# Beginning of a six-layer local-attention kernel: clearings, mask, x copies, softplus and input statistics placed elsewhere

## What is computed

```
xn = (x - mean) / sqrt(var + 1e-5)
s  = recurrent_branch(xn)            # log_alpha = -8 * softplus(forget_base) * sigmoid(forget)
for i in range(6):
    t = attn(shift_tokens(t), Wqkv[i], ...) + t    # 16 heads of 64, window 32, masked softmax
    t = ffn(shift_tokens(t), ...) + t              # layer norm, gated GELU
out = x + s * silu(t)
```

## Time and profile before

| what | value |
|---|---|
| median of three runs | 1648.02 us |
| the profiled execution | 1647.35 us |
| its span in the profile | 1645.6 us |
| busy: PE, PEld | 97%, 83% |
| busy: DVE, ACT, POOL | 83%, 82%, 80% |
| mean granted clock of TensorE | 0.998 of full speed |
| the chain that ended last | PE 81%, DVE 7%, ACT 4%, POOL 3%, issue 3% |

### The profile page before, as it was taken

One profiled execution on the slowest core, in us unless ns is written; L12 is line 12 of the kernel. 1 busy time (PEld: TensorE's weight loads), 2 busy tenths in 40 slices (PEclk: granted clock), 3 DMA queues, 4 the chain that ended last, 5 costly groups with the idle time before them and its releaser, 6 DMA issues.

```text
span 1645.6 us, 50851 instructions
## 1 busy us (share of the span) xinstructions
PE 1592.4 (97%) x19920; PEld 1367.4 (83%) x19920; DVE 1368.5 (83%) x2011; ACT 1343.9 (82%) x2518; POOL 1322.8 (80%) x1283
## 2 busy tenths in 40 slices
PE   5899999999999999999999999999999999999997
PEld 3678888888888888888888888888888888888786
DVE  6888888888888888888888888888888888888865
ACT  5768888788888888888888888888888888878884
POOL 8988898888889888889888889878888776677742
PEclk9999999999999999999999999999999999999999
DMA  4345233433323344232344333334333332222231
GB/s 135 99 119 140 71 98 85 119 108 98 107 76 90 102 116 120 77 106 76 100 113 114 99 83 99 84 105 132 86 94 87 92 85 69 77 73 69 64 113 33
DMA packets 184871, 156.89 MB, mean 95 GB/s; under 512 B 111550, under 2 KB 156092, under 8 KB 184636
## 3 DMA queue, kind: packets, MB, share of 16 engines
q1 hardware_dynamic: 184636, 153.64, 33.4%
HBM read 27.56 MB, written 1.05 MB: 17 GB/s over the span
## 4 chain that ended last, share of the span: by engine, by line
PE 81%; DVE 7%; ACT 4%; POOL 3%; issue 3%; DMA 0%; SPq 0%; POOLq 0%; ACTq 0%; DVEq 0%
PE ps_pv L793 12%; PE ps_s L769 10%; PE ps_pv L812 9%; PE ps_tr L730 9%; PE ps_qn L702 8%; PE ps_qn L703 7%; PE ps_qn L704 7%; PE ps_tr L714 5%; PE ps_pv L802 3%; PE ps_s L752 2%; PE ps_qn L892 2%; PE ps_qn L893 2%; PE ps_qn L894 2%; DVE ss L1542 1%; POOL qk L1968 1%
## 5 line engine op out<-in xcount | busy, mean ns | idle before, releaser
L1968 POOL TENSOR_TENSOR qk<-qk,t 128x1024 f32<-128x1024 f32 x192 | 455.8, 2376 | 92.8 <-DVE qk L1532 92.6
L1529 DVE TENSOR_TENSOR t<-ps_qn,tab 128x512 f32<-128x512 f32 x384 | 264.6, 689 | 129.3 <-ACT sq L1128 116.4
L1980 POOL TENSOR_TENSOR qkr<-qk,rinv 128x1024 f32<-128x1024 f32 x192 | 361.7, 1905 | 7.7 <-POOL rinv L1960 0.4
L1115 ACT ACTIVATE pbd<-ps_tr 64x512 f32<-64x512 f32 x384 | 226.0, 589 | 63.9 <-PE ps_tr L714 60.9
L702 PE MATMUL ps_qn<-w_hi,xs_hi 128*128 128x512 f32 x576 | 260.3, 452 | 16.4 <-DVE qk L1532 7.5
L1532 DVE TENSOR_TENSOR qk<-ps_qn,tab 128x512 f32<-128x512 f32 x384 | 261.5, 681 | 0.0
L1128 ACT ACTIVATE sq<-ps_qn 128x512 f32<-128x512 f32 x384 | 228.6, 596 | 35.8 <-PE ps_qn L704 31.1
L1161 ACT ACTIVATE qbd<-ps_tr 64x512 f32<-64x512 f32 x384 | 226.8, 591 | 32.7 <-PE ps_tr L730 27.2
L703 PE MATMUL ps_qn<-w_lo,xs_hi 128*128 128x512 f32 x576 | 229.2, 398 | 0.0
L704 PE MATMUL ps_qn<-w_hi,xs_lo 128*128 128x512 f32 x576 | 228.6, 397 | 0.0
L1542 DVE TENSOR_REDUCE ss<-sq 128x32 f32<-128x2048 f32 x96 | 216.6, 2256 | 0.0
(11 more groups left out here) (168 smaller groups left out, 3206.1 us busy)
## 6 DMA issues: line engine op xcount, KB each, us to landing
v_own<-v_new SPq DMA_DIRECT2D x96, 512.0 KB, 3.2
v_back<-v_new SPq DMA_DIRECT2D x96, 384.0 KB, 3.5
v_back<-v_own SPq DMA_DIRECT2D x94, 128.0 KB, 2.3
kT<-kT SPq DMA_DIRECT2D x84, 128.0 KB, 2.7
w_raw<-in_Wqkv SPq DMA_DIRECT2D x18, 512.0 KB, 5.2
rot<-in_rot SPq DMA_DIRECT2D x48, 128.0 KB, 2.6
fx<-xmid SPq DMA_DIRECT2D x96, 64.0 KB, 2.1
xsh<-x SPq DMA_DIRECT2D x190, 32.0 KB, 2.6
```

What stands on the lines that cost most here:

```text
L1529: v.tensor_tensor(t2[:, part].rearrange("p (h s d) -> p h s d", s=2, d=DH // 2), swapped, tab[:, 2 * k + 1:2 * k + 2, :].rearrange("p o (s ...
L1968: g.tensor_tensor(qk[b][:, part], qk[b][:, part], t2[:, part], ALU.add).then_inc(added[b], 1)
L1980: g.tensor_tensor(qkr[b][:, part].rearrange("p (h d) -> p h d", d=DH), qk[b][:, part].rearrange("p (h d) -> p h d", d=DH), rinv[b][:, k * ...
```

## The change

What it does:
- **Loads.** x comes in three parts instead of two: tiles 0 and 1 first as before, tiles 2 and 3 before the weights, tiles 4 to 7 between the k and the v part. The rotary table and the scales are issued before the k part instead of behind it.
- **Input statistics.** Columns 4 to 7 are taken after the first moments and before `input_root(0)`; columns 8 to 11 after the second rotation of half (0,0); columns 12 to 15 at the end of (0,0), with the moments of all twelve there as before.
- **x copies.** `copy_pair` is ScalarE's instead of VectorE's: pair 0 in (1,0) before `normalise_pair(1)`, pair 1 in (1,1) at the same place, pair 2 at the end of (1,1).
- **Mask.** The two conversions to bf16 are done by ScalarE in (0,1) (`round_mask`, after the copies of values) instead of by GpSimd in (0,0).
- **Clearings.** `clear_recurrent` follows `clear`, before GpSimd's first `split_first`.
- **Softplus.** Its size is taken by GpSimd at the end of (2,1) instead of (0,1), its exponential by ScalarE in (3,0) instead of (1,0), its reciprocals by VectorE in (3,1) instead of (1,1).

```diff
-        x_in, ... = [sem(f"x_loaded{q}") for q in range(2)], ...
+        x_in, ... = [sem(f"x_loaded{q}") for q in range(3)], ...
...
                 load_x(0, 2, 0)
                 sp.dma_start(rec.par[:, :, :], a["rec_par"]).then_inc(rec_par_in, 16)
                 sp.dma_start(ident[:, :], a["ident"]).then_inc(s_const, 16)
+                load_x(2, 4, 1)
                 w.load_wqkv(sp, 0, 0)
-                w.load_wqkv(sp, 0, 1)
                 w.load_rot(sp, 0)
                 w.load_scales(sp, 0)
+                w.load_wqkv(sp, 0, 1)
+                load_x(4, TILES, 2)
                 w.load_wqkv(sp, 0, 2)
-                load_x(2, TILES, 1)
...
# ScalarE
-                    act.wait_ge(s_st, 2 * (HEAD if g == 0 else COLUMNS))
+                    act.wait_ge(s_st, 2 * (COLUMNS if g else HEAD))
...
+                def copy_pair(r):
+                    bank, tokens = in_pair(r)
+                    act.wait_ge(s_tr, HEAD * (r + 2))
+                    f(x[:, :, tokens].rearrange("p b (t d) -> p t b d", d=P),
+                      bank[:, :].rearrange("p (t b d) -> p t b d", t=2, b=B), ACT.Copy).then_inc(s_xT, 1)
...
+                def round_mask():
+                    act.wait_ge(mask_in, 2 * 16)
+                    f(mask_bf[:, :, :], fc[:, :, :], ACT.Copy).then_inc(mask_ready, 1)
+                    f(sel_bf[:, :], fsq[:, 0, :], ACT.Copy).then_inc(mask_ready, 1)
...
                     if (i.n, b) == (1, 0):
+                        copy_pair(0)
                         normalise_pair(1)
+                    if (i.n, b) == (3, 0):
                         softplus_exp()
+                    if (i.n, b) == (1, 1):
+                        copy_pair(1)
...
+                    if (i.n, b) == (0, 1):
+                        round_mask()
                     if (i.n, b) in ((0, 1), (1, 0)):
                         normalise_pair(2 * i.n)
+                    if (i.n, b) == (1, 1):
+                        copy_pair(2)
...
# VectorE
-                    dve.wait_ge(s_st, 2 * (HEAD if g == 0 else COLUMNS))
+                    dve.wait_ge(s_st, 2 * COLUMNS if g else 3 * HEAD)
...
+                        if i.first and (b, c) == (0, 1):
+                            input_stats(range(8, 12), 2)
...
-                    if (i.n, b) == (1, 1):
-                        copy_pair(1)
+                    if (i.n, b) == (3, 1):
                         softplus_recip()
...
-                        input_stats(range(HEAD, COLUMNS), 1)
+                        input_stats(range(12, COLUMNS), 2)
                         input_moments(range(HEAD, COLUMNS), HEAD + COLUMNS)
-                    elif (i.n, b) == (1, 0):
-                        square_sums(i, b)
-                        copy_pair(0)
...
-                    if (i.n, b) == (1, 1):
-                        copy_pair(2)
...
                 input_stats(range(HEAD), 0)
                 input_moments(range(HEAD), HEAD)
+                input_stats(range(HEAD, 8), 1)
                 input_root(0)
...
# GpSimd
-                    if (i.n, b) == (0, 0):
-                        mask_constants_bf()
-                    elif (i.n, b) == (0, 1):
+                    if (i.n, b) == (2, 1):
                         softplus_size()
-                        clear_recurrent()
...
                 clear()
+                clear_recurrent()
                 for c in range(3):
                     split_first(c)
```

More of the change, by code:

```diff
@@ L430, in layers @@
         HEAD, COLUMNS = 4, B * TILES
-        x_in, s_const, s_set, rec_cleared = [sem(f"x_loaded{q}") for q in range(2)], sem("ident_loaded"), sem("constants_set"), sem("rec_cleared")
+        x_in, s_const, s_set, rec_cleared = [sem(f"x_loaded{q}") for q in range(3)], sem("ident_loaded"), sem("constants_set"), sem("rec_cleared")
         s_st, s_ln, s_y0, s_nw, s_xn, s_tr, s_xT = map(sem, (
@@ L1773, in copy_head @@
                         v.tensor_copy(x[:, :, 1 + P:1 + 2 * P], ps_pv[0][:, 0:B * P].rearrange("p (b t) -> p b t", b=B)).then_inc(s_xT, 1)
[L1775 to L1779, removed]
                 def low_first_x():
@@ L2094, in split_first @@
                                     ALU.subtract).then_inc(lo_ready[part] if c % 2 or part == 2 else first_low, 1)
[L2096 to L2099, removed]
                 def clear_recurrent():
```

## The result

The changed kernel takes 1649.75 us, the median of 20 runs (1648.44 to 1652.18), against 1647.89 us for the kernel before, also of 20 (1646.86 to 1649.75). The ratio is 1.0014, with a 95% interval of 1.0007 to 1.002: 1.9 us slower, where 1.1 was forecast, and inside the 0.2% that was called no change. The profiled execution took 1649.03 us with a span of 1647.2, 1.6 longer than before.

The account below looks back on a forecast made before the run. GpSimd works almost without a gap, with ScalarE only 0.19 us from being the bound at one place. Terms: +1.1 - 0.2 - 0.19 + 0.4 = +1.1 us, giving 1649.1 us; range 1646.3 to 1651.2.

Parts of the forecast that it names:

- ScalarE is the next bound in (1,0): In the third half step, ScalarE's continuous work was to keep GpSimd's 2.45 us gain from being passed on.
- The sign that was named: Before GpSimd's Newton step of (1,1): idle 2 us or more, released by ScalarE's root L1176, ScalarE itself not waiting.
- Rival (a): GpSimd's relief counts in (1,0): its earlier adds pull ScalarE's work in, the 2.45 us stand, total 1646.4; chance 18%.
- Floor -0.19: GpSimd's earlier floor of (0,1) saves only the 0.19 us that ScalarE's root of (1,0) waited for GpSimd's floor.
- copy +0.4 less the exponential: In (1,0) ScalarE gains copy_pair(0), 0.54 us, and loses the softplus exponential, 0.1: sum +0.4 us.
- The start, +1.1: Later q and k weights and four statistics ahead of the input root shift the start by 1.1 us.
- about 8.0: Forecast landing time in us of the q weights, which landed at 7.0 before and are issued 0.98 later.
- Root ... +0.9: At the start, input_root(0) waits for the new x and four statistics: from 6.01 to 6.9 us, +0.9.
- (b): Rival: the loads at the start don't queue, so the shift is 0.6 instead of 1.1, total 1648.6; chance 17%.
- (c): Rival: k weights wait behind the scales and land at 13.4, third split +2.9 us, total 1650.9; chance 12%.
- Statistics: -0.2: Four instead of twelve statistics at the end of (0,0) let GpSimd's add of keys in (0,1) gain 0.2 us.
- Clearings, mask, softplus, copies of (1,1): nothing: These moved parts fall into waits of their engines, in the first two steps and later, and cost nothing.

Follow-up runs that it names:

- gaps kernels: ScalarE normalises pairs 1 and 2 in its waits for TensorE: on the kernel before with only GpSimd's three parts moved, 1645.84 us; on the changed kernel, 1647.51 us.
- Relief only: Kernel before with only clearings, mask and softplus moved as in the change; loads, statistics and x copies as before: 1647.11 us, ratio 0.9997.
- changed kernel, again: The changed kernel, unedited, run once more for a second profile: 1649.49 us, ratio 1.0013.
- loads only: Kernel before with only SyncE's new order of loads; later statistics stay at the end of (0,0): 1649.65 us, ratio 1.001.
- kernel before, again: The kernel before, unedited, run once more for a second profile: 1646.69 us, one run.
- copies back: The changed kernel with all three x pair copies on VectorE again at their old places: 1648.28 us, ratio 1.0004.
- changed, gaps used: The changed kernel with ScalarE's normalisation of pairs 1 and 2 moved into its gaps behind the second squares: 1647.51 us, ratio 1.0.
- old start, again: Repeat of the changed kernel with loads and input statistics as in the kernel before: 1648.05 us, ratio 1.0005.
- start mended: The changed kernel with q, k, rotary table, scales loaded as before, then x tiles 2 and 3, v, remaining x; statistics 4 to 7 later: 1648.08 us.
- old start: The changed kernel with loads and input statistics as in the kernel before, first run: 1648.59 us, ratio 1.0006.
- start mended, gaps used: The changed kernel with mended loads and statistics, pairs 1 and 2 normalised in ScalarE's gaps, mask and pair 0 normalisation earlier: 1645.50 us, ratio 0.9987.
- the next kernel: Start mended, gaps used, but with x pair 0 copied by VectorE at its old place: 1644.82 us, ratio 0.9987.

## Why the prediction was right, and where it was off

1. **ScalarE is the next bound in (1,0): right.** The sign that was named, GpSimd idle 2 us or more, released by ScalarE's root, with ScalarE not waiting, stands there with 3.15. That the relief itself was there is shown by the gaps kernels, which let it through (2.08 and 2.55 in the stretch). In the repeat of the kernel before even the 0.19 was gone: ScalarE and GpSimd were both the bound there. Rival (a), in which GpSimd's earlier adds would pull ScalarE along, is out: the stretch didn't shrink.
2. **Floor -0.19, copy +0.4 less the exponential: right.** Relief only: 13.18, that is 0.37 less than before. Of this 0.09 is the exponential, and 0.28 lies between the start of the last normalisation and the root (1.82 before, 1.54 now): the wait printed as 0.19, and the 0.1 by which the records of neighbours overlap where there is no wait. The copy added 0.46; the step was sized 0.54 less 0.1.
3. **The start, +1.1: the direction was right, the term too small.** In nine executions with the old order of q and k the third `w_hi` stood between 9.92 and 10.49, 10.1 on average; in five with the new loads between 11.40 and 12.46, 11.8 on average: +1.7 (+1.6 without the 12.46 of the changed kernel, again). Two sizes failed. q was given "about 8.0", its old landing time and the later issue; it landed at 8.7, 5.0 from its issue in place of 4.3 (4.9 in loads only, 4.7 in the changed kernel, again; 4.1 in the kernel before, again). That the x ahead of it slowed it is the likely reason, not a shown one. And the earlier trace rows were of an execution whose first x came late, at 3.98 where eleven of the other thirteen had 3.39 to 3.70, so the start of before was 0.45 later in it than in its repeat. The step "Root ... +0.9" named the wrong term for this profile: the input root was delayed by 0.86, but loads only shows the same third w_hi with that root at 5.60. The weights set it there, as in copies back and in changed, gaps used, where ScalarE's first `w_hi` waited 0.20 and 0.62 for them. In the changed kernel, again, the step was right: x came last, and the start moved by 0.7 more. k at 11.7 was as forecast (11.6), just as ScalarE came to it; rivals (b) and (c) are out.
4. **The Trainium skill's DMA cost** (DMA: Bandwidth & Descriptors, fixed and variable cost) gives 3.2 us for each 512 KB; the page fits it to transfers that GpSimd issues, and these are SyncE's. The measured 5.0, 6.6 and 8.0 are further from it than the 4.3, 5.1 and 7.8 before, with two more transfers ahead of q and four more ahead of k and v.
5. **Statistics: -0.2.** Moments ended at 25.0 (24.7 forecast). VectorE then waited 1.13 for the square, and the add of keys that had waited 0.20 ran without a gap. The +1.28 of the root of (0,0) against before became +1.03 at the next root: 0.25 gained, as forecast. Between the two repeats it is 0.14 (12.21 to 12.07).
6. **Clearings, mask, softplus, copies of (1,1): nothing, right by the profile.** The clearings ended at 7.26, 2.2 before the first `w_lo`. From (1,0)'s root to (1,1)'s took 13.65 (13.68 before), with two copies more on ScalarE, which still waited 2.49 for the earlier trace rows's 2.98. The mask took ScalarE's wait ahead of the root of (0,1) in relief only, where that root stood 0.28 behind the floor; in the changed kernel 0.37 of wait was left. It cost nothing behind: from the last copy of values to the first copy of keys relief only took 8.06 us, and the kernel before, again, 8.07. What stays open is the medians' 1.2 to 1.5 for the three copies, of which the profiles place 0.46 in (1,0), nothing in (1,1), and at most the 0.27 of (3,1) below.
7. **The end.** At 62 us the changed profile was 1.11 behind, as the sum had it, but that is partly luck: the kernel before was 0.71 earlier there in its repeat, and the changed kernel 0.50 later in its own. Averaged over the two executions of each, the distance is 1.7 at 62 us and 2.1 at the last root; so some 0.3 to 0.4 comes in small steps later. The largest, 0.27, is in (3,1). In loads only VectorE waits there for a transfer that landed 4.3 us after its issue (3.8 in the kernel before, again), as its timeline shows:

```profile
119.31 1.29 DVE L1554 COPY v_new<-ps_qn 128x512 f32<-128x512 f32 x2 [1.24 <-DMA v_own<-v_new]
```
In the changed kernel and in old start, again, ScalarE's first copy of probabilities starts 1.67 us after the root, not 1.41, though the transpositions ahead of it start as soon after the root as before (0.65). Relief only and the kernel before again have neither. The softplus reciprocals, moved into this half, take 0.28 of VectorE there in relief only, and are lost in a wait for TensorE. Why an unchanged half takes longer when the copies are ScalarE's or the loads are new is open.

So the forecast of +1.1 was 0.8 short of the measured 1.9 (in times, 1649.1 for 1649.75). By the profiles, the load order was worth about 1.7 at the start instead of 1.1, and 0.3 to 0.4 was lost later in places priced at nothing; the copy's 0.4 and the two small gains stood as sized. The medians divide the loss otherwise (1.0 to 1.1 for the start by taking it out, 1.2 to 1.5 for the copies), and their intervals are too wide to say which account is closer.

## What to carry to other kernels

When an engine is relieved, find the instruction of another engine that it waits for next, and read how long that engine waits before it: the relief is worth no more than that (0.19 here, 0.04 in a repeat), until the second engine's own work is moved into its gaps. An early transfer put ahead of the one that everything waits for can delay it by more than its issue (here q was issued 0.98 us later and landed 1.7 later): price the queue at the landing that ends the wait, and check whether the earlier data is needed sooner at all. A start read off one execution can be off by half a microsecond, so take it from two before a term of that size is built on it.

## What the runs showed of the hardware

The stretch in which TensorE was granted half its clock (its lower level, 1.2 GHz) doesn't stay in its place. The kernel before was at it in 22 to 26 us in one execution, and in the other, of the same instructions, in 16 to 20 and from 26 on. Here first the other execution, then the one known so far:

```profile
16.00:20.00 4.00, 3.45 (x10) 2.00 (x8) 4.00 (x6) 1.42 (x4) 4.00 (x3) 0.57 0.03 8
22.00:26.00 4.00, 1.83 (x9) 1.12 (x7) 3.96 (x22) 2.08 (x7) 3.66 (x8) 1.00 0.87 273
26.00:36.00 10.00, 8.14 (x19) 4.40 (x17) 6.31 (x12) 5.18 (x12) 9.29 (x13) 0.52 0.29 91
```
```profile
16.00:20.00 4.00, 3.60 (x11) 2.29 (x11) 3.10 (x6) 1.73 (x4) 3.56 (x3) 1.00 0.00 0
22.00:26.00 4.00, 2.91 (x6) 1.82 (x6) 3.97 (x26) 1.66 (x5) 3.57 (x9) 0.57 0.82 244
26.00:36.00 10.00, 5.77 (x20) 3.08 (x20) 6.96 (x14) 5.67 (x16) 9.47 (x12) 1.00 0.37 116
```
The column of the clock doesn't show all of it. From 14 to 16 us it reads 1.00 in both executions, but six 128x512 matmuls that begin there took 0.63 us or more each in the first profile and 0.39 to 0.47 in the repeat. The first line is of the kernel before, the second of its repeat:

```profile
15.18 0.63 PE L703 MATMUL ps_qn<-w_lo,xs_hi 128*128 128x512 f32 x1
```
```profile
14.49 0.40 PE L703 MATMUL ps_qn<-w_lo,xs_hi 128*128 128x512 f32 x1
```
All fourteen profiles fall into two groups by this. Where these six took 0.63 or more, which is what such matmuls take where the column reads half (at 22 to 24 us in the first profile), ScalarE's root of (0,0) came 12.30 to 12.34 us after the third `w_hi` (eight profiles, the first ones of both kernels among them); where they took 0.39 to 0.47 it came 11.85 to 11.94 after it (six profiles, with the repeats of both). So a slow stretch there costs about 0.4 us, although TensorE has room. Each kernel's first profile is in one group and its repeat in the other, so the comparisons of both above are even in this. Later, from 26 to 36 us, it cost something too: the kernel before took 12.03 from the root of (0,0) to that of (0,1) at full clock there and 12.21 at half, and start mended, which has other edits too, took 12.75 at half from 16 to 36. In (1,0) it lengthened ScalarE's stretch by 1.3 us in old start (14.94 for 13.64, at half for part of 38 to 44) and by 1.1 in start mended, gaps used (12.19 for the 11.11 of the next kernel, 34 to 42). Three profiles of single variants were misleading for that reason, and only a repeat or the median of 11 runs put them right.

The first x landed at times between 3.39 and 3.98 us from execution to execution, without a change in what was ahead of it. The second pair, issued at 2.7, landed between 5.80 and 5.99 in three executions with the statistics ahead of the input root, and at 7.07 in a fourth.
